# Linear attention over three pairs at once: the second unit's norm, Wo and placing a step later, and sorted places for 16 tiles at a time

## The reference, cut to what matters

```
def _L1_attn_ref(x, ...):                  # C = 128, H = 16 heads, K = 2
    q  = x + x @ Wq.T + bq
    ks = x[None] + jnp.einsum('bnc,kdc->kbnd', x, Wk) + bk
    vs = x[None] + jnp.einsum('bnc,kdc->kbnd', x, Wv) + bv
    q, ks = silu(q) + 0.5, silu(ks) + 0.5
    q  = q / (norm(q) + 1e-6);  ks = ks / (norm(ks) + 1e-6)      # per head
    states = jnp.einsum('kbhnd,kbhne->kbhde', ks * scale, vs * scale)
    out = jnp.einsum('bhnd,bhde->bhne', q, jnp.prod(states, axis=0))
    out = (out - mu) * rsqrt(var + 1e-5) * ln_g + ln_b
    return out @ Wo.T + bo
def _L1_ffn_ref(x, ...):                   # 32 experts, I = 256
    shared_out = (silu(x @ sg) * (x @ su)) @ sd
    topk_ids = jnp.argmax(x @ gate_w, axis=-1)
    order = jnp.argsort(topk_ids)          # tokens sorted by expert
    routed_out = grouped_swiglu(xs[order], ...)[argsort(order)]
    return shared_out + routed_out
x = x + s * silu(g)
```

## Time and profile before

| | |
|---|---|
| median of 3 runs | 1456.67 us (1455.31 to 1457.17) |
| profiled execution | 1457.29 us, its span 1455.5 us |
| mean granted TensorE clock | 0.923 |
| busy share of the span | PE 84%, DVE 70%, ACT 54%, POOL 45% |
| `stage3_mix` | 943.8 to 1255.9 us, 21% of the span |

### The profile page before, as it was taken

The page is one execution under the profiler, slowest core; times in us unless marked ns, Lnnn a source line. Parts: engine busy times, 40 slices in busy tenths (PEclk is TensorE's granted clock), DMA queues, the critical chain, the costliest instruction groups (busy, mean ns, idle before and its releaser), DMA issues. The chain is left out here.

```text
span 1455.5 us, 29222 instructions
## 1 busy us (share of the span) xinstructions
PE 1217.5 (84%) x7815; PEld 920.2 (63%) x7816; DVE 1018.3 (70%) x3639; ACT 783.6 (54%) x2010; POOL 653.9 (45%) x1270
## 2 busy tenths in 40 slices
PE   3999999999935999999999555588888888599993
PEld 2778787777724677777777444356666666366662
DVE  2777777777777677777776388667777777266663
ACT  1675756566622656656566366556666666233331
POOL 2343434344221555545555378614444444146665
PEclk9999999999967999999999755589999999799997
DMA  3424333333311222222222166534444444355562
GB/s 138 152 93 141 100 132 115 116 130 101 115 42 30 41 60 47 54 58 41 58 47 49 35 191 215 166 111 151 148 147 149 148 148 140 110 154 175 176 181 71
DMA packets 159257, 162.84 MB, mean 112 GB/s; under 512 B 20950, under 2 KB 138429, under 8 KB 159216
## 3 DMA queue, kind: packets, MB, share of 16 engines
q1 hardware_dynamic: 143936, 133.23, 29.3%
q0 software_dynamic: 14848, 26.77, 6.7%
q10 hardware_dynamic: 432, 2.38, 0.4%
HBM read 76.59 MB, written 71.04 MB: 101 GB/s over the span
## 5 line engine op out<-in xcount | busy, mean ns | idle before, releaser
L392 ACT ACTIVATE pr<-ps,nmx 128x256 f32<-128x256 f32 x256 | 117.7, 472 | 44.6 <-DVE nmx L439 44.0
L380 ACT ACTIVATE big<-ps,BHS 128x256 f32<-128x256 f32 x256 | 107.0, 470 | 62.2 <-PE ps L257 61.5
L257 PE MATMUL ps<-big,W 128*128 128x256 f32 x512 | 131.8, 403 | 5.9 <-ACT big L385 5.9
L270 PE MATMUL ps<-W,big 128*128 128x128 f32 x1024 | 130.7, 281 | 0.0
L270 PEld LDWEIGHTS ps<-W,big 128*128 128x128 f32 x1024 | 119.6, 192 | 13.9 <-ACT big L380 9.9
L2144 POOL DMA_INDIRECT out<-X,io x96 | 100.4, 1046 | 34.4 <-issue 34.4
L257 PEld LDWEIGHTS ps<-big,W 128*128 128x128 f32 x512 | 96.4, 198 | 27.8 <-ACT big L385 16.3
L439 DVE TENSOR_REDUCE nmx<-ps 128x2 f32<-128x512 f32 x128 | 82.5, 686 | 39.6 <-PE ps L292 38.9
L1986 PE MATMUL ps<-big,zT 128*128 x192 | 101.9, 613 | 8.5 <-DVE pr L2082 8.3
L1007 POOL DMA_INDIRECT ffn<-big,si x64 | 94.0, 1468 | 26.6 <-issue 26.6
L2060 ACT ACTIVATE pr<-ps 128x256 f32<-128x256 f32 x96 | 36.8, 383 | 106.6 <-PE ps L1986 106.6
(11 more groups left out here) (256 smaller groups left out, 3302.4 us busy)
## 6 DMA issues: line engine op xcount, KB each, us to landing
srt<-big SPq DMA_DIRECT2D x16, 1584.0 KB, 5.8
X<-srt SPq DMA_DIRECT2D x24, 800.0 KB
big<-we SPq DMA_DIRECT2D x16, 768.0 KB, 4.9
rowd<-big SPq DMA_DIRECT2D x32, 272.0 KB, 2.2
big<-x SPq DMA_DIRECT2D x64, 128.0 KB, 2.2
X<-big SPq DMA_DIRECT2D x64, 128.0 KB, 2.1
big<-we SPq DMA_DIRECT2D x16, 384.0 KB, 3.6
X<-srt SPq DMA_DIRECT2D x24, 256.0 KB, 3.0
```

The source lines that it names most:

```text
L257: last = pe.matmul(pb[2 * g + f // 2][:, f % 2 * S:(f % 2 + 1) * S], W0[:, l, 512 + f * P:512 + (f + 1) * P], zT2[:, g, :], start=True, st ...
L270: last = pe.matmul(pb[4 + g][:, t * C:(t + 1) * C], hT[:, g, f, t * P:(t + 1) * P], W0[:, l, 1024 + f * C:1024 + (f + 1) * C], start=(f == ...
L380: act.activation(hT[:, g, f, :], pb[2 * g + half][:, f % 2 * S:(f % 2 + 1) * S], ACT.Silu, bias=BHS[:, l, f:f + 1], scale=GELU).then_inc(s ...
L392: last = act.activation(pr[:, g, h, t, :], pb[2 * g + h][:, t * S:(t + 1) * S], ACT.Exp, bias=nmx[:, g, h * TPU + t:h * TPU + t + 1], accu ...
```

## The change

The work of a pair is spread over three steps. In `step(i)` (now with flags `begin`, `cont`, `end`) stand the early part of pair i, the middle of pair i - 1, and the end of pair i - 2: for unit 1 `norm`, `turn`, `affine`, `out` and `result`, and for both units `place`. `roots` stands at the end of the step in which the squares are summed and no longer at the start of the next; `bias` is cut into `values` (second v) and the rest; PSUM banks 6 and 7 get other users. There is one more step at the end (i = 17). SP asks for x of unit 1 a step later than for unit 0. The sorted places are computed by `slots(k)` for a quarter of the tiles (16) at once into `IX`: three passes over 16 x 32 = 512 elements and one over 16; k = 0 and 1 ahead of step 0, 2 in step 0, 3 in step 1. In each step a copy of 4 values to `ix[m]` is left (`slots_of`).

```diff
                 # bodies3
-                step(0, 1, -1, late=False)
-                step(1, 0, 0)
+                step(0, 1, -1, -1, cont=False, end=False)
+                step(1, 0, 0, -1, end=False)
                 with engine.Fori(1, HALF // 2) as r:
                     for m in range(2):
-                        step(2 * r + m, 1 - m, r - 1 + m)
-                step(HALF, 1, HALF // 2 - 1, early=False)
+                        step(2 * r + m, 1 - m, r - 1 + m, r - 1)
+                step(HALF, 1, HALF // 2 - 1, HALF // 2 - 1, begin=False)
+                step(HALF + 1, 0, HALF // 2, HALF // 2 - 1, begin=False, cont=False)
...
                 # SP
+                        if not first:
+                            sp.wait_ge(s["gu"], 2 * i)
+                            turned(i, 1)
...
-                        for g in range(2):
-                            if not last:
-                                sp.wait_ge(s["gu"], 2 * i + g + 1)
-                                turned(i + 1, g)
+                        if not last:
+                            sp.wait_ge(s["gu"], 2 * i + 1)
+                            turned(i + 1, 0)
...
                 # POOL
+                        if end:
                             for g in range(2):
-                                rstd(i, g)
+                                place(i - 2, 1 - m, rt, g)
+                        if cont:
                             for g in range(2):
-                                place(i, m, r, g)
+                                rstd(i - 1, g)
...
                 # PE, the new step
+                        if cont:
+                            hidden(p, 1)
+                            if end:
+                                pe.wait_ge(s["sh"], 2 * p)
+                            shared(p, 0, 6)
...
+                        if end:
+                            pe.wait_ge(s["s1"], 2 * p + 1)
+                            turn(p - 1, 1, 7)
+                        if begin:
+                            if cont:
+                                pe.wait_ge(s["sh"], 2 * p + 1)
                             project(i, 0, 6)
+                        if end:
+                            out(p - 1, 1, 7)
+                        if cont:
+                            states(p, 0)
+                            pe.wait_ge(s["s1"], 2 * p + 2)
+                            queries(p, 0, 7)
+                            states(p, 1)
+                            pe.wait_ge(s["qT"], 2 * p + 1)
+                            queries(p, 1, 7)
+                            attention(p, 0)
...
                 # DVE
+                    def slots(k):
+                        n = NT // 4
...
+                        q = slice(n * k, n * (k + 1))
+                        dve.tensor_tensor(eq, EID[:, q].unsqueeze(2).to_broadcast([P, n, E1]),
+                                          CST[:, C_IOTA:C_IOTA + E1].unsqueeze(1).to_broadcast([P, n, E1]), ALU.is_equal)
+                        dve.drain()
+                        dve.tensor_tensor(at_, eq, off[:, :].unsqueeze(1).to_broadcast([P, n, E1]), ALU.mult)
+                        dve.drain()
+                        dve.tensor_reduce(sl[:, :], at_, X_AXIS, ALU.add)
+                        dve.drain()
+                        dve.tensor_tensor(IX[:, q], sl[:, :], RNK[:, q], ALU.add)
...
+                        if end:
+                            result(p - 1, 1 - m, rt, 0, 7)
+                        if cont:
+                            normed(p)
+                        if cont and not end:
+                            slots(3)
+                        if end:
+                            result(p - 1, 1 - m, rt, 1, 7)
+                        if cont:
+                            gated(p, 1)
+                        if begin:
+                            if cont:
+                                dve.wait_ge(s["states"], 2 * p + 1)
+                            dve.wait_ge(s["proj"], 2 * i + 1)
+                            values(i, 0, 6)
+                        if cont:
+                            state(p, 0)
+                        if begin:
+                            if cont:
+                                dve.wait_ge(s["qTp"], 2 * p + 1)
+                            bias(i, 0)
...
```

More of the change, by code:

```diff
@@ L1567, in rows, with step @@
                           .then_inc(row_in[m][g], 16)
-                    def step(i, m, r, last=False):
+                    def step(i, m, r, first=False, last=False):
+                        if not first:
+                            sp.wait_ge(s["gu"], 2 * i)
+                            turned(i, 1)
                         sp.dma_start(big[:, bass.ds(n_w * i, n_w)], we1[:, bass.ds(n_w * i, n_w)]).then_inc(we1_in, 16)
@@ L1580, in _ @@
                     for m in range(2):
-                        step(m, m, 0)
+                        step(m, m, 0, m == 0)
                     with sp.Fori(1, HALF // 2 - 1) as r:
@@ L1585, in _ @@
                     for m in range(2):
-                        step(HALF - 2 + m, m, HALF // 2 - 1, m == 1)
+                        step(HALF - 2 + m, m, HALF // 2 - 1, last=m == 1)
                     sp.wait_ge(we1_in, 16 * HALF)
@@ L1686, in table, with step @@
                         pe.matmul(pb[0][0:1, 0:P], tef[:, :], ident, start=True, stop=True).then_inc(s["table"], 1)
[L1688 to L1700, removed]
-                            project(i, 0, 6)
[L1702 to L1710, removed]
+                    def step(i, m, r, rt, begin=True, cont=True, end=True):
+                        p = i - 1
+                        if cont:
[3 more added lines that the diff above has]
+                            shared(p, 0, 6)
+                            if not begin:
+                                table()
+                        if end:
[4 more added lines that the diff above has]
+                                pe.wait_ge(s["sh"], 2 * p + 1)
+                            project(i, 0, 6)
+                        if end:
[10 more added lines that the diff above has]
+                            if cont:
+                                pe.wait_ge(s["hmul"], 2 * p + 2)
+                            else:
+                                pe.wait_ge(s["vb"], 1)
@@ L1729, in _ @@
+                            shared(p, 1, 6)
+                            out(p, 0, 7)
                     pe.matmul(pb[7][:, 0:E1], ONES[:, :], cum[:, 0, :], start=True, stop=True).then_inc(s["table"], 1)
@@ L1764, in norm, with affine, step @@
                         last.then_inc(s["z2"], 1)
-                    def affine(i, g, b):
-                        act.wait_ge(s["zTp"], 2 * (i - 1) + g + 1)
+                    def affine(p, g, b):
+                        act.wait_ge(s["zTp"], 2 * p + g + 1)
                         act.activation(zT[:, g, :], pb[b][:, half], ACT.Identity, bias=lb, scale=ls).then_inc(s["zT"], 1)
[L1770 to L1776, removed]
-                            rooted(i, 0)
[L1778 to L1782, removed]
-                            rooted(i, 1)
-                        if late:
-                            norm(i, 1)
-                        if early:
+                    def step(i, m, r, rt, begin=True, cont=True, end=True):
+                        p = i - 1
+                        if end:
+                            norm(p - 1, 1)
+                        if cont:
+                            shared(p, m, r, 0, 6)
+                        if end:
+                            affine(p - 1, 1, 7)
+                        if cont:
+                            gate(p, 1)
+                            queries(p, 0, 7)
+                        if begin:
+                            rooted(i, 0)
+                            squared(0)
+                        if cont:
+                            queries(p, 1, 7)
+                            norm(p, 0)
+                        if begin:
+                            rooted(i, 1)
+                        if cont:
+                            affine(p, 0, 7)
+                        if begin:
+                            squared(1)
+                        if cont:
+                            shared(p, m, r, 1, 6)
+                        if begin:
@@ L1787, in step @@
                             gate(i, 0)
[L1788 to L1791, removed]
+                            roots(i)
                     act.activation(carrier_a[:, 1:2], PHALF[:, 0:1], ACT.Copy).then_inc(s["z2"], 2)
@@ L1909, in step @@
                             squares(i, 1)
                             gated(i, 0)
-                        if late:
-                            result(i, m, r, 1, 7)
                     dve.memset(sl[:, :], 0.0).then_inc(s["s1"], 2)
                     offsets()
+                    for k in range(2):
+                        slots(k)
                     bodies3(dve, step)
```

168 lines of the change are left out of this document (85 added, 83 removed).

## The result

The changed kernel takes 1441.67 us (median of 4 runs, 1440.95 to 1444.25), the kernel before 1455.99 beside it (4 runs, 1454.9 to 1457.17): a ratio of 0.9901 with an interval of 0.9886 to 0.9916. It is faster, by half of what was forecast, and 0.7 us above the range. Its profiled execution took 1442.23 us, span 1440.4, against 1457.3 of before.

What follows compares the result with a forecast made beforehand. No engine was full, so a chain through the engines of 18.15 us a step set the pace; 31.5 us gained less 2.9 lost is 28.6 off 1457.3, 1428.7, forecast as 1429 us, range 1421 to 1441.

Steps and rivals of the forecast that it cites:

- The walk: Loop of `stage3_mix`: longest way round the new ScalarE and PE lists, a step of 16.05 us, 2.1 us less.
- The gain between norm and silu and between squares and load: ScalarE, loop: norm to silu 1.80 us becomes 0.69; squares to load 2.17 becomes 0.39 + 0.49.
- `rstd` 1133.37 to 1135.33, 1.96: 4.96: POOL, unit 0: `rstd` start to norm's start takes 1.96 us as in the old order, bringing the running sum to 4.96.
- Room of 0.8 us, so nothing there: POOL: placing, now ahead of `rstd`, finishes before unit 0's statistics end with 0.8 us to spare, so costs nothing.
- The end of the stage: Last of 15 steps from bias of pair 1, without early work: gains 2.1 us; extra step 17 costs nothing.
- The slots: VectorE: removing 64 small instructions saves nothing; four batches at 2.6 us each, partly covered, lose 2.9 us (2.0 to 4.5).
- rival 1: Loop: step shrinks half as much, a side branch (`normed` or second load) bounding; 16.9 us a step, 1441 us; chance 0.22.
- the second load: ScalarE side branch, table load back to silu: 3.3 to 3.7 us beside 4.06 + 0.34, 0.7 us of room.
- Rival 2: Loop: step shrinks more, as PE's 2.26 project or POOL's 1.96 may shrink; 15.5 us a step, 1420 us; chance 0.11.
- Rival 3: SP's queue: placing delays x for unit 0; decides from a 9 us landing, at 12 a 1474 us time; chance 0.02.
- The table load: ScalarE: a switch costs 1.30 us; the skill's 1.38 us drain per load would give 1439 us, left out of the sum.

## Why the prediction was wrong

**The round.** The walk came to 16.05 us, and its order holds: with `rstd` at its true length, 16.05 + (2.84 - 1.96) = 16.93, measured 16.88. With the drains out it is 1.49 (1114.89 to the norm at 1116.38), the walk gives 15.58, and 15.78 was measured, with TensorE busy 96 of 100 us. The gain between norm and silu and between squares and load was real: from norm to silu it is 0.70 us (1141.95 to 1142.65), from squares to load 1.71 (1144.03 to 1145.74), where the walk has 0.69 and 1.72.

**The step that failed** is the term "`rstd` 1133.37 to 1135.33, 1.96: 4.96". It was taken over from a place where no transfer of POOL was under way into one where four had just been issued, and this although a part further down moved the placing there and costed it with "Room of 0.8 us, so nothing there". The room was right (0.96); the nothing was not. The 1.96 held two drains, and what a drain waits for depends on what stands ahead of it: 0.50 us there, 1.2 to 2.1 here. Against the walk the fourteen steps lose 14 x 0.83 = 11.6 us of the 13.5 that the profiled execution missed its forecast by.

**The end of the stage** was to gain a step's 2.1 us and lost 0.15: 2.25 short. The head, 0.2 better than forecast, and the stretches outside the stage, 0.15 less, bring the sum to the 13.5. With `rstd` free of drains and one ahead of placing, the end is 31.3 us (1186.87 to 1218.13) for 34.8 before. In the changed kernel `rstd` waits 1.67 us there, and TensorE, idle meanwhile, is at a clock of 0.53 from 1224 to 1240. How much of the 3.7 us between the two is the drain and how much the clock was not told apart.

**The slots** were to cost 2.9 us, with the head: measured 2.7, with the batches at 2.55 each, where 2.6 was taken. That these meet is in part luck, since the changed kernel had the higher clock in its head (0.68 for 0.61); at a like clock the batches cost about 3.6. That the old slots cost nothing is confirmed: over the fourteen steps it is 16.79 us with them and 16.88 without.

**The rivals.** The time fell on rival 1's 1441 at 16.9 a step, but not by its mechanism: neither `normed` nor the second load bounds at 16.9, since the step falls to 15.78 with both in place. Rival 2 named POOL's 1.96, but as a piece that may shrink; it grew, and only without drains is it shorter. Rival 3 did not come; the landing grew from 2.9 to 4.0 us, far from 9.

**The table load.** In the changed kernel a load takes 1.28 us and begins 0.01 us behind the gate ahead of it (1145.14 + 0.59, 1145.74). The Trainium skill (ScalarE: Activation LUTs, What ACT_TABLE_LOAD costs) adds a drain of about 1.38 us to each, which made 1439 in the forecast, near the measured time. That the numbers meet is chance. The kernel without drains on POOL has as many loads and a step of 15.78, below the walk that had no such drain; by the rule it would be 0.7 above it.

## What to carry to other kernels

A drain on POOL cost here what was still under way of its indirect transfers, and a little for each that had landed, so its time is no property of the block it stands in: when a schedule moves it behind an issue, price it anew. In this kernel it paid to order small dependent instructions on POOL by a semaphore, and to put one drain where the engine waits anyway. Work moved out of a loop pays only if the loop had no room for it; here it moved from cover into the open.

## What was not expected of the hardware

- A drain on POOL behind four indirect transfers of 128 rows let it go on 3.7 us after the last issue's start: 2.78 us of idle time directly behind them, 1.2 to 2.1 (mostly 1.4) some 1.3 us later, 0.3 to 0.5 when they had long landed.
- Landed transfers that no drain has met are not free: with none in the stage its end took 5.55 us for 2.30, and a single drain 5.24, with no packet moving. By these it is 0.085 to 0.09 us each (an estimate).
- A semaphore between two small instructions on POOL left 0.1 us between them (1115.05 + 0.21 to 1115.35), a drain at best about 0.15.
